# VectorE transposes, w_in copies on ScalarE, and a patch-by-patch table in a two-part convolution kernel

## The reference

```
x = x + L0(_gn(x))     # six depthwise experts, three chosen per image; part one of the kernel
x = x + L1(_gn(x))     # part two, the one that is changed:

h  = einsum('oc,bchw->bohw', w_in, x)            # 32 -> 170 channels
xf = rfft2(8x8 patches of h) * fft_filter        # per channel filter in each patch
h  = irfft2(xf), patches put back
y  = depthwise 3x3 convolution of h, padding SAME
g  = gelu(y[:, :85]) * y[:, 85:]
out = einsum('oc,bchw->bohw', w_out, g)          # 85 -> 32 channels
```

## Time and profile before

| | |
|---|---|
| median of 3 runs | 3818.72 us (3818.24 to 3818.98) |
| profiled execution, its own time | 3803.13 us |
| its span, first to last instruction | 3801.1 us |
| granted TensorE clock, mean | 0.977 |
| TensorE matmul busy | 3188.2 us, 84% |
| TensorE weight load busy | 2278.3 us, 60% |
| VectorE busy | 2054.9 us, 54% |
| ScalarE busy | 1586.3 us, 42% |

### The profile page before, as it was taken

The page is one execution under the profiler, slowest core; times in us unless marked ns, Lnnn a source line. Parts: engine busy times, 40 slices in busy tenths (PEclk is TensorE's granted clock), DMA queues, the critical chain, the costliest instruction groups (busy, mean ns, idle before and its releaser), DMA issues.

```text
span 3801.1 us, 192863 instructions
## 1 busy us (share of the span) xinstructions
PE 3188.2 (84%) x88198; PEld 2278.3 (60%) x88198; DVE 2054.9 (54%) x4198; ACT 1586.3 (42%) x2217; POOL 252.5 (7%) x274
## 2 busy tenths in 40 slices
PE   5699999999968888888888888888888888888887
PEld 4355555454536666666666666666666666666665
DVE  3365656566524555555555555555555555555554
ACT  1244434343423444444444444444444444444443
POOL 2011111111111000000000000000000000000000
PEclk9999999999976999999999999999999999999999
DMA  6677777787651333333333333333333333333332
GB/s 127 133 169 170 168 169 166 167 174 166 137 70 42 94 84 82 89 95 100 96 78 82 92 103 97 88 78 82 90 99 96 94 78 84 94 100 97 87 81 74
DMA packets 452132, 406.01 MB, mean 107 GB/s; under 512 B 404233, under 2 KB 404539, under 8 KB 447558
## 3 DMA queue, kind: packets, MB, share of 16 engines
q1 hardware_dynamic: 446092, 376.96, 43.0%
q10 hardware_dynamic: 5228, 16.70, 1.2%
HBM read 165.80 MB, written 78.16 MB: 64 GB/s over the span
## 4 chain that ended last, share of the span: by engine, by line
PE 53%; issue 7%; DVE 4%; ACT 3%; DMA 3%; ACTq 1%; SPq 0%; POOL 0%; POOLq 0%
PE ps L1323 12%; PE ps L1305 11%; PE ps L1255 9%; PE ps L1290 9%; PE ps L1273 7%; PE ps L1335 4%; DMA neighbours<-border 3%; DVE gated L1385 2%; ACT gelu L1189 2%; ACTq L1199 1%; DVE channels_first L1173 1%; ACT channels_first L1173 1%; DVE border L1165 1%; SPq L1054 0%; ACT border L1165 0%
## 5 line engine op out<-in xcount | busy, mean ns | idle before, releaser
L449 ACT ACTIVATE hidden<-ps,hidden_scale 128x576 f32<-128x576 f32 x512 | 351.2, 737 | 614.2 <-PE ps L554 614.2
L1385 DVE TENSOR_TENSOR gated<-gelu,ps 128x432 f32<-128x432 f32 (+1 forms) x512 | 290.1, 567 | 548.9 <-ACT gelu L1189 522.4
L1323 PE MATMUL ps<-ident,gated 64*44 64x64 f32 x18432 | 480.2, 246 | 89.8 <-issue 75.3
L1323 PEld LDWEIGHTS ps<-ident,gated 64*44 64x44 f32 x18432 | 425.3, 172 | 136.5 <-issue 90.5
L1165 ACT COPY border<-ps 128x432 f32<-128x432 f32 (+1 forms) x512 | 226.2, 494 | 635.3 <-PE ps L1273 215.5
L1290 PE MATMUL ps<-hidden_patches,channel_tables 64*64 64x144 f32 x11264 | 403.7, 287 | 96.1 <-DVE gated L1385 96.1
L1155 DVE COPY hidden_patches<-ps 128x704 f32<-128x704 f32 x288 | 390.3, 1355 | 160.1 <-PE ps L1255 154.9
L1273 PE MATMUL ps<-hidden_patches,channel_tables 64*64 64x144 f32 x11264 | 403.0, 287 | 86.8 <-DVE border L1165 85.2
L568 PE MATMUL ps<-hidden,taps 128*32 128x288 f32 x6144 | 436.3, 416 | 42.1 <-DMA taps<-conv_tables 27.4
L1155 ACT COPY hidden_patches<-ps 128x704 f32<-128x704 f32 x288 | 394.6, 1370 | 175.7 <-PE ps L1255 175.6
L1255 PE MATMUL ps<-w_in_t,x_normed 32*64 32x88 f32 x18432 | 404.0, 246 | 76.0 <-issue 66.0
(11 more groups left out here) (151 smaller groups left out, 1956.8 us busy)
## 6 DMA issues: line engine op xcount, KB each, us to landing
neighbours<-border SPq DMA_DIRECT2D x1024, 126.8 KB
taps<-conv_tables SPq DMA_DIRECT2D x192, 216.0 KB
x_image<-in_x_dram SPq DMA_DIRECT2D x128, 288.0 KB, 5.7
x<-x_image SPq DMA_DIRECT2D x128, 288.0 KB, 4.8
x_image<-x SPq DMA_DIRECT2D x384, 96.0 KB
out_dram<-x_image SPq DMA_DIRECT2D x384, 96.0 KB, 2.0
x_rows<-in_x_dram SPq DMA_DIRECT2D x512, 60.0 KB
neighbours<-border ACTq DMA_DIRECT2D x1024, 15.8 KB
```

Source lines behind the costliest of these rows:

```text
L449: A(hid[T % 3][:, 2 * h:2 * h + 2, :, 1:1 + W], ps1[:, 2 * h:2 * h + 2, 0:XB * W].rearrange("p c (k w) -> p c k w", k=XB), ACT.Relu, scale ...
L1323: last = MM(ps[NV * x:NV * x + NT4, odd, o:o + NV], gt[r, :, n], ident[r, :], start=True, stop=True)
L1385: TT(o, gl[odd][:, 0:n * NPC].rearrange("p (t m) -> p t m", m=NPC), ps[:, 2 * odd + 1, 0:n * NPC].rearrange("p (t m) -> p t m", m=NPC), AL ...
```

## The change

The transposes leave TensorE. VectorE transposes 32 x 32 blocks of `gated` straight from SBUF into `channels_first`, two instructions per step, each 128 partitions x 512 elements: the first takes channels 0 to 31 of the 44, the second channels 12 to 43 (the overlap meets zero rows in the weights). w_out therefore takes two accumulating matmuls where it took one, with the weights laid out in four pieces, and there is no identity any more. The copies out of PSUM of the transposed patches are gone. ScalarE makes all copies from w_in, both pairs. `hidden_patches` becomes `[P, NPC, NCH]`: a patch's 88 channels side by side, so that these copies write adjacent floats, and border and hidden read their 144 moving columns with a step of 88 floats. w_out of step v is now issued in step v, right behind w_in.

```diff
-        U = sb("hidden_patches", [P, NCH, NPC])
+        U = sb("hidden_patches", [P, NPC, NCH])
-        wo = sb("w_out_t", [P, 2, C])
+        wo = sb("w_out_t", [P, 2, 2, C])
...
+        SB = 32
...
-                for odd in range(2):
-                    for x in range(2):
-                        out_half = x ^ odd
-                        g = NT4 * out_half
-                        n = min(NT4, HID - g)
-                        sp.dma_start(wo[NV * x:NV * x + n, odd, :], w_out.rearrange("c o -> o c")[g:g + n, :]).then_inc(s_ow, 16)
+                for h in range(2):
+                    n = min(NT4, HID - NT4 * h) - SB
+                    for b in range(2):
+                        o = NV * h + SB * b
+                        sp.dma_start(wo[o:o + SB, b, 0, :], w_out.rearrange("c o -> o c")[NT4 * h:NT4 * h + SB, :]).then_inc(s_ow, 16)
+                        o += 2 * SB - NT4
+                        sp.dma_start(wo[o:o + n, b, 1, :], w_out.rearrange("c o -> o c")[NT4 * h + SB:NT4 * h + SB + n, :]).then_inc(s_ow, 16)
             sp.dma_start(sel[:, :], select_c.ap()).then_inc(s_ow, 16)
-            sp.dma_start(ident[:, :], eye_c.ap()).then_inc(s_ow, 16)
...
-        def w_in_copy(eng, copy, pair, k, v):
+        def w_in_copy(pair, k, v):
-            eng.wait_ge(s_w, 2 * (NW * k + v) + pair + 1)
-            o = U.rearrange("p c (q n) -> p q n c", q=NQUAD)[:, 2 * pair:2 * pair + 2, WSTEP * v:WSTEP * v + WSTEP, :]
+            nc.scalar.wait_ge(s_w, 2 * (NW * k + v) + pair + 1)
+            o = U.rearrange("p (q n) c -> p q n c", q=NQUAD)[:, 2 * pair:2 * pair + 2, WSTEP * v:WSTEP * v + WSTEP, :]
             i = ps[:, 4 + 2 * pair:6 + 2 * pair, 0:WSTEP * NCH].rearrange("p q (n c) -> p q n c", c=NCH)
-            copy(o, i).then_inc(s_we[pair], 1)
+            nc.scalar.copy(o, i).then_inc(s_we[pair], 1)
...
-        def transposed_copy(eng, copy, x, k, v):
-
-            j, r = NW * k + v, slice(NV * x, NV * x + NT4)
-            eng.wait_ge(s_t, j + 1)
-            need(eng, s_wo, j - 1)
-            copy(ct[j % 2][r, :], ps[r, 0:2, :].rearrange("p a b -> p (a b)")).then_inc(s_te[x], 1)
-
...
-                    if k < B:
-                        w_in_copy(act, nc.scalar.copy, 0, k, v)
-                    if k > 0:
-                        transposed_copy(act, nc.scalar.copy, 0, k - 1, v)
+                    for pair in range(2):
+                        if k < B:
+                            w_in_copy(pair, k, v)
...
-                                last = MM(ps[half(h ^ y), 4 + i, o:o + NPC], tbl[half(h), j, NV:2 * NV], U[half(h), j, :],
+                                last = MM(ps[half(h ^ y), 4 + i, o:o + NPC], tbl[half(h), j, NV:2 * NV], U[half(h), :, j],
...
-                                last = MM(ps[half(h ^ odd), i, o:o + NPC], tbl[half(h), j, 0:NV], U[half(h), j, :],
+                                last = MM(ps[half(h ^ odd), i, o:o + NPC], tbl[half(h), j, 0:NV], U[half(h), :, j],
...
-            def transposes(k, v):
+            def w_out_step(k, v):
 
                 j = NW * k + v
-                if v == 0:
-                    pe.wait_ge(s_m, 2 * NSETS * (k + 1))
-                need(pe, s_te[0], j)
-                need(pe, s_te[1], j)
...
-                pe.wait_ge(s_te[0], j + 1)
-                pe.wait_ge(s_te[1], j + 1)
+                pe.wait_ge(s_te, j + 1)
                 need(pe, s_r, j - 1)
...
+                t = ct[j % 2].rearrange("p (s n) -> p s n", s=2)
+                for b in range(2):
+                    for s in range(2):
+                        for q in range(NQUAD):
+                            o = ps[C * q:C * q + C, 2 + j % 2, 0:WSTEP * NV].rearrange("p (i b n) -> p b i n", i=WSTEP, b=2)[:, b]
+                            last = MM(o, wo[:, b, s, :], t[:, s, P * q:P * q + P], start=(s == 0), stop=(s == 1),
+                                      skip_group_check=True)
                 last.then_inc(s_wo, 1)
...
                     if k > 0:
-                        transposes(k - 1, v)
-                        if v > 0:
-                            w_out_step(k - 1, v - 1)
-                if k > 0:
-                    w_out_step(k - 1, NW - 1)
+                        w_out_step(k - 1, v)
...
+            def transposes(k, v):
+
+                j = NW * k + v
+                if v == 0:
+                    dve.wait_ge(s_m, 2 * NSETS * (k + 1))
+                need(dve, s_wo, j - 1)
+                t = ct[j % 2].rearrange("p (s q i n) -> p s q i n", s=2, q=NQUAD, i=WSTEP)
+                for s in range(2):
+                    first = s * (NT4 - SB)
+                    g = gt[:, first:first + SB, :].rearrange("p t (q i) -> p q i t", q=NQUAD)[:, :, WSTEP * v:WSTEP * v + WSTEP, :]
+                    last = nc.vector.transpose(t[:, s], g)
+                last.then_inc(s_te, 1)
...
-                    if k < B:
-                        w_in_copy(dve, TC, 1, k, v)
                     if k > 0:
-                        transposed_copy(dve, TC, 1, k - 1, v)
+                        transposes(k - 1, v)
+                    if k > 0:
                         if v > 0:
                             residual(k - 1, v - 1)
```

More of the change, by code:

```diff
@@ L953, in filter_part @@
     select_c = inl(border_select(), "border_select")
-    eye_c = inl(np.tile(np.eye(NV), (2, 1)), "eye2")
     x1v = x1.ap().rearrange("g (b c) (q t) -> (g b) q c t", b=IMG, q=NQUAD)
@@ L974, in filter_part @@
         xn = sb("x1_normed", [P, PXQ])
-        ident = sb("ident2", [P, NV])
         sel = sb("select", [P, NV])
         wi = sb("w_in_t", [P, NCOL])
-        wo = sb("w_out_t", [P, 2, C])
+        wo = sb("w_out_t", [P, 2, 2, C])
         nrm = sb("norm_scale_bias", [P, B, 2])
@@ L1012, in filter_part @@
         s_m = sem("gated_done")
-        s_t = sem("transposed")
-        s_te = [sem(f"transposed_copied{i}") for i in range(2)]
+        s_te = sem("transposed")
         s_wo = sem("w_out_done")
@@ L1129, in _ @@
             MS(ct[1][:, :], 0.0)
-            MS(wo[:, :, :], 0.0).then_inc(s_z, 1)
+            MS(wo[:, :, :, :], 0.0).then_inc(s_z, 1)
             pool.wait_ge(s_z, 1)
@@ L1307, in add_neighbours @@
                     last.then_inc(s_y, 1)
-            def transposes(k, v):
-                j = NW * k + v
-                if v == 0:
-                    pe.wait_ge(s_m, 2 * NSETS * (k + 1))
-                need(pe, s_te[0], j)
-                need(pe, s_te[1], j)
[L1316 to L1324, removed]
             def w_out_step(k, v):
                 j = NW * k + v
-                pe.wait_ge(s_te[0], j + 1)
-                pe.wait_ge(s_te[1], j + 1)
+                pe.wait_ge(s_te, j + 1)
                 need(pe, s_r, j - 1)
[L1332 to L1335, removed]
+                t = ct[j % 2].rearrange("p (s n) -> p s n", s=2)
[5 more added lines that the diff above has]
+                                      skip_group_check=True)
                 last.then_inc(s_wo, 1)
-            pe.wait_ge(s_ow, 16 * 6)
+            pe.wait_ge(s_ow, 16 * 9)
             for k in range(B + 1):
@@ L1382, in gate @@
                 if s == 0:
-                    need(dve, s_t, NW * k)
+                    need(dve, s_te, NW * k)
                 o = gt.rearrange("p (t s) n -> p t s n", s=2)[:, CUT[s]:CUT[s + 1], odd, :]
```

## The result

The changed kernel takes 4699.36 us, median of 4 runs (4692.49 to 4719.71), against 3818.85 us: a ratio of 1.231, 95% interval 1.228 to 1.235. That is 881 us slower, where 224 were forecast. The profiled execution took 4692.49 us, its span 4690.5 us.

The account below looks back on a forecast made before the run. TensorE bounds the kernel, limited by instruction supply around w_in and w_out. Those save 390 us, border and hidden's strided reads add 614: net +224 on the profiled 3801.1, 4027, median 4043 us; 8-in-10 range 3670 to 4540.

Parts of the forecast that it names:

- part 3: Border and hidden reading moving columns 88 floats apart: 1.68 ns a column, +120 ns a group, +19.3 us an image.
- Rival (c): Border and hidden's strided read slower still, two corners sharing a read path: 2.2 ns a column, 4430 us; chance 0.10.
- (e): In border and hidden, a float read twice per column: 3.4 ns, 59 us an image, 5300 us; chance 0.02.
- The path through stage B: Border, hidden and neighbours, 42.9 us an image: TensorE nearly end to end, so slower reads add 19.3 us.
- the cover of the DMA: Border 2 and hidden 0 ended 0.72 us before the border rows' DMA; growing 1.44 each, they add 2.0 us.
- Part 1: Between w_in and w_out, transposes move from TensorE to VectorE: 1.02 us each, step 2.65 us, 12.3 us an image saved.
- (a): Border and hidden's strided read is free, TensorE reading far enough ahead: 0.85 ns a column, 3429 us; chance 0.12.
- (b): Border and hidden's strided read is partly hidden: 1.2 ns a column, 8.0 us an image, 3685 us; chance 0.16.
- (d): VectorE's transposes between w_in and w_out take 1.9 us each, a step 4.4 us: 4530 us; chance 0.06.
- Part 2: ScalarE's w_in copies, written side by side: 0.75 us each, hidden; gains 7 us in image 0, 2 after the last.
- Stage A's saving: w_in and w_out with the transposes, 38.8 us an image, become 26.5; in all 390 us less.
- Instruction supply: In w_in, transposes and w_out, TensorE is limited by how fast instructions arrive, about 256 per 4 us.

Follow-up runs that it names:

- adjacent_read: The changed kernel, but border and hidden read 144 adjacent floats of the same table (wrong values, same work): 3458.53 us.
- table_only: The kernel before with only hidden_patches laid out patch by patch, transposes staying on TensorE: 5070.52 us.

## Why the prediction was wrong

**The sign was right, the size was not**: +224 forecast, +881 measured, outside the range of 3670 to 4540.

**The term that failed is part 3's price of a column.** The prediction took 1.68 ns from three engines' strided rows and called them evidence for a step of 88 floats. They all stem from a step of 144. The blocks show that 144, 96, 112 and 16 cost 1.7 ns, just as read, but 88 costs 2.5. The group grew by 360 - 122 = 238 ns where +120 was put: 39.6 us an image in place of 19.3. No row of the trace of before has this step; the error was to give "strided" a single price and to bound it above by 2.2 ns from a weight load with another step. Rival (c) had a similar size (2.2 ns, +31 us an image, 4430) for a wrong reason, and (e), the same floats read twice, went past it.

**The path through stage B held.** Its terms as listed add up to 19.7 us and not 19.3, a slip of addition. With 238 ns a group in place of 120 the same terms give 5.7 + 4.8 + 17.1 + 8.9 + 3.8 = 40.3 us, an estimate; 39.6 were measured. With a step that does cost 1.7 ns for border, the kernel pays 21.9 us an image, 2.2 more than those 19.7. Hidden at 3.3 instead of 2.94 us for 48 accounts for it: 0.36 for each of six sets of three slots and 0.24 for each of two sets of two on the path are 2.6. So the cover of the DMA was used up and the gate waits absorbed about as worked out. Rows 8 misled the rivals: L513's excess of 0.4 ns a column came from 16 columns; the block at its step of 4 floats has 1.8 ns, 0.95 over adjacent ones.

**Part 1's price held, its step did not.** The transposes take 1.035 us against 1.02 taken, and rivals (a), (b) and (d) are out. But VectorE is not the longest in stage A. Its records overlap a little, two transposes last 1.98 us together, and its step is 2.2 us where 2.65 was put:

```profile
2380.02 0.37 DVE L1380 TENSOR_TENSOR x_image<-ps,x_image 128x256 f32<-128x256 f32 x1
2380.32 1.98 DVE L1369 STREAM_TRANSPOSE channels_first<-gated 128x512 f32<-128x512 f32 x2
2382.23 0.37 DVE L1380 TENSOR_TENSOR x_image<-ps,x_image 128x256 f32<-128x256 f32 x1
```

On the chain of waits of stage A, TensorE follows TensorE from the first w_out on, broken only by "issue" pieces and, at the end, by ScalarE's last copies. Its step is 1.17 + 1.01 = 2.18 us, and 3.9 at the lower clock:

```profile
2595.93 1.87 PE ps L1309 x32
2597.80 2.05 PE ps L1245 x64
...
2604.77 1.17 PE ps L1245 x59
2605.95 1.01 PE ps L1309 x32
```

**Part 2 held**: 0.749 us against 0.75, off the path.

**Stage A's saving was forecast 45 us too large**: 344.6 in adjacent_read and not 390. Some 24 us of this lie in the kernel before: the prediction took 38.8 us from one image, and the mean of 31 is 38.0. The new stage A has the forecast's 26.5 us as its mean in the changed kernel (27.0 in adjacent_read), but that was luck. It is made of other terms: 9 x 2.18 = 19.6 us of TensorE's work, 1.9 of waiting for the first transposes, 2.2 of "issue" and, as an estimate, 1.4 lost to the lower clock (half of the 2.9 us spent at it), 25.1 of the 26.5. The prediction counted 1.0 us until the last gates, and did not say what TensorE does while it waits for the first transposes, nor that w_in can run at half the clock behind that. With w_in ahead, stage A is 2.3 and 2.7 us shorter in two kernels. In the changed kernel 1.3 us less idle time and, by the same estimate, 1.2 us of the clock cover its 2.3. That the wait brings on the lower clock isn't shown: the same wait is followed by the full clock in 13 of 31 images.

**Instruction supply** stays an inference. "Issue" pieces stay when the copies become cheap (table_only, stage A no shorter), and this idle time fell from 5.1 to 2.2 us an image in stage A with the transposes off TensorE, as was forecast. Both speak for it; no run changed the supply itself.

## What to carry to other kernels

A step through SBUF has no single price: take it from a row with the same step, or measure that step by itself, before a table is laid out by it. Two adjacent floats are enough: a table in pairs made both the write and the read cheap (0.78 us, and 1.53 against 1.47), where laying it out wholly for one side cost the other 1234 us. Take a stage's length from all its images and not from one. And when work leaves the bounding engine for another, ask what the first does while it waits for the first result.

## What the runs showed of the hardware

- The price of a moving column at float32, 144 columns, four corners: 0.85 ns adjacent, about the same at step 2 (block 1.79 us against 1.70), 1.8 ns at step 4, 1.7 ns at 16, 32, 48, 64, 80, 96, 112 and 144 floats, and 2.5 ns at 24, 88 and 152. 24, 88 and 152 differ by 64 floats (256 bytes), and so do 4 and 68, 12 and 76, 20 and 84, 40 and 104, 56 and 120, 72 and 136; the blocks of each pair agree within 0.02 us. Why it is so is open.
- It holds for one corner alone as for four, and for the whole array in float32 (24 records at step 88: 8.87 us, at step 4: 6.39, at step 1: 3.21). In bfloat16 on the whole array, 24 records take 2.86 us at step 1, 6.30 at step 8 and 6.49 at step 88. Those two steps are 16 and 176 bytes, that is 4 and 44 floats, so no block in bfloat16 has the 352 bytes of float32's step 88. The granted clock of these three blocks was 0.57, 0.74 and 0.50.
- Wide steps cost the same at both levels of the clock: 48 border records at step 88 took 4.56 us at a granted clock of 0.50 and 4.51 us at 1.00, where with adjacent columns they take 3.16 us at the lower one and 1.70 us at the upper one on the same kind of timeline.
- Two streams over the same partitions cost more at some steps when they are less than 4 floats apart (1 apart against 44: step 96, 3.48 against 3.15 us; step 64, 3.93 against 3.16), and step 96 also at 64 floats apart (3.51). At step 88 they cost nothing more at any distance tried.
- VectorE's transpose of 128x512 float32, read with a step of 144 floats, is 1035 ns, close to what a strided copy's slope gives (1.02 us); the lower bound of 0.69 us was not tried with adjacent reads.
